# Moving the feature additions of an expert-routing stage, and one of three normalising steps of the last stage, to other engines

## The chip, the cores and the metric

The kernel runs on one core of a Trainium2 chip. Its time is the device time in microseconds of one execution. Three executions of the kernel before took 1827.47, 1829.99 and 1833.80 us, so the median is 1829.99 us. Engines are named as in the profile: PE is TensorE, DVE is VectorE, ACT is ScalarE, POOL is GpSimd, SP is SyncE. SP issues transfers only.

## What is computed

The input x is [8, 1024, 128] in float32: 8 batches of 1024 tokens. Two layers follow each other. Layer 0 is a recurrent mixer and a mixture of 8 experts. Layer 1 is a linear attention of three layers and a feed-forward part whose weight matrix depends on the token's position. The change touches the end of the two feed-forward parts. What they compute, shortened:

```
# layer 0, second half
h = layernorm(x) * (1 + cb) + sb                     # "feats"
eid   = argmax(h @ centroids.T)                      # the expert of each token
alpha = sigmoid(h @ centroids[e])
y     = h + relu(norm(h) @ w1[e] + b1[e]) @ w2[e] + b2[e]
x = x + gb * (alpha * y + (1 - alpha) * h)           # = x + gb*h + gb*alpha*(expert part)

# layer 1, second half
h = layernorm(x) * (1 + cb) + sb
idx = argmax over 8 tiles of the position scores     # one tile index for each position
y = h @ W[idx].T + b[idx]
x = x + gb * y
```

The term gb*h of the first half is the one that the change moves. It is independent of the experts' result, and is added to x in SBUF.

## The kernel before, in words

A batch is 8 chunks of 128 tokens (partition = token, 128 elements = channel). A half is 4 chunks, a tile of 128x512 elements. There are 16 halves.

**The expert stage**, function `experts`, is written out engine by engine in one block. The program on each engine is a fixed sequence. Engines meet only in semaphores. It has three phases:

- *Routing*, ten turns (b from -2 to 7), three batches in flight. PE turns the normalised rows (L1155) and computes affinities and transposes them back (L1162, L1164). ACT writes the features to `ex_feats` (L1105) and the normalised feature rows into a row buffer `ex_rows` (L1098). DVE picks the expert of each token and its place in a sorted list (L923 to L945). In each turn DVE also computes a shift (L905) for which ACT waits before L1098, copies gates (L918), and adds the features of half 0 of the batch before to x: `features_summed` (L950, L951). POOL scatters the rows of each batch to DRAM with eight indirect transfers (L1049).
- *The tile table.* From the final counts DVE computes which expert and which rows each of 71 tiles has (L980 to L998). At L987 it releases SP, which writes eight padding blocks (L1226), waits until all of these and all scatters have landed, and then loads one tile after another (L1234).
- *The tile loop*, 71 tiles. PE turns a tile (L1184), ACT scales it (L1132), PE multiplies by w1 (L1192) and w2 (L1199), ACT and DVE apply the ReLU (L1141, L1008), DVE forms the result (L1017, L1018), and POOL stores it by an indirect transfer (L1058). For each tile DVE copies the w1 of its expert into `ex_fT` (L1004) and thereby releases PE's L1192. The expert numbers come from registers that DVE loads from the table, 24 at a time.

Between table and loop DVE copies two w1 blocks and then does the other nine `features_summed`: half 1 of each batch, and half 0 of the last.

**The last stage**, inside `attention`, works on 8 batches of 10 rows of chunks (`ti_rows`), each in three parts of 4, 3 and 3 chunks (`PARTS`). ACT computes the reciprocal deviation of the next batch (L361, L362), DVE the shift (L1452), and ACT normalises the next batch's chunks in place, part after part (L1637), between its own modulations of the present batch (L1647). PE turns each part (L1902) and multiplies by the position's weights (L1914). DVE adds the bias (L1467) and computes the statistics of the batch after next (L1442, L1447). POOL scales the result (L1776), SP stores it, POOL gathers it back (L1783).

## Time and profile before

| | |
|---|---|
| time of the three executions | 1827.47, 1829.99, 1833.80 us |
| time of the profiled execution | 1829.99 us |
| its span, first to last instruction | 1828.0 us |
| PE busy | 1571.7 us (86%) |
| DVE busy | 1443.5 us (79%) |
| ACT busy | 935.3 us (51%) |
| POOL busy | 698.6 us (38%) |
| mean granted TensorE clock | 0.916 of full speed |

The profiled execution took the median time, and 1.99 us of it lie outside the span. The routing phase runs from about 213 to 333 us of the span, the tile loop from 356.9 to about 499 us, the attention until about 1742 us, and the last stage to the end. In a row of the timeline the first number is the start in us from the span's start and the second the busy time in us. At the end stands in brackets how long the engine was idle before it, and what released it. Busy time includes the time for which an instruction, once issued, is held up inside its engine.

### The profile page before, as it was taken

Reading aid. Unit: us, or ns where it says so; the run is one execution under the profiler, and the core shown is the slowest. Engines: PE = TensorE matmul, PEld = TensorE weight load, DVE = VectorE, ACT = ScalarE, POOL = GpSimd, SP = SyncE. Lnnn points to the kernel's source line nnn. Section 1 sums busy time; section 2 is a strip of 40 time slices with the busy share of each in tenths; the row PEclk is TensorE's granted clock in tenths of the full one; section 3 lists DMA queues with packets and bytes.
Section 4 is the critical chain, followed back from the end, with each engine's and each line's share of the span. In section 5 each row is a group of like instructions: output and inputs, shape, how many; then the busy total and the mean of one; then the engine's idle time right before and its main releaser. Section 6 shows DMA issues by size and latency. Waiting matters only on the chain.

```text
span 1828.0 us, 65037 instructions
## 1 busy us (share of the span) xinstructions
PE 1571.7 (86%) x27934; PEld 1150.5 (63%) x27934; DVE 1443.5 (79%) x3906; ACT 935.3 (51%) x1958; POOL 698.6 (38%) x620
## 2 busy tenths in 40 slices
PE   6777365399969999999999999999999999999853
PEld 4344254399946677776667777666677667777542
DVE  4998566766658888888888888888888988888864
ACT  4887476366524444445544444554444544444373
POOL 0777636345513234215224323423321522431354
PEclk9888655599969999999999999999999999999876
DMA  9730012333200000000000000100000000000437
GB/s 264 145 100 1 21 50 90 97 102 101 83 13 14 3 9 9 15 3 14 15 3 13 16 3 8 20 3 9 9 15 3 14 15 3 11 6 3 109 102 233
DMA packets 88606, 79.69 MB, mean 44 GB/s; under 512 B 22416, under 2 KB 77040, under 8 KB 88064
## 3 DMA queue, kind: packets, MB, share of 16 engines
q1 hardware_dynamic: 70736, 46.17, 9.6%
q0 software_dynamic: 10848, 25.70, 4.9%
q8 instruction: 221, 3.62, 0.9%
q10 hardware_dynamic: 6736, 3.66, 0.7%
q14 instruction: 65, 0.53, 0.1%
HBM read 46.74 MB, written 34.01 MB: 44 GB/s over the span
## 4 chain that ended last, share of the span: by engine, by line
PE 50%; DVE 13%; ACT 4%; issue 2%; DMA 1%; DVEq 1%; POOL 0%; another core or an unknown queue 0%; POOLq 0%; ACTq 0%
PE psum L1965 8%; PE psum L1890 8%; PE psum L1859 4%; PE psum L1868 4%; PE psum L1928 2%; PE psum L1934 2%; PE psum L1882 2%; PE psum L1936 2%; PE psum L1875 2%; PE psum L1937 2%; PE psum L1938 2%; PE psum L1948 2%; PE psum L1847 2%; DVE at_kb L1543 2%; PE psum L1929 2%
## 5 line engine op out<-in xcount | busy, mean ns | idle before, releaser
L1890 PE MATMUL psum<-attn_w,at_qa 128*128 128x128 f32 x1536 | 197.6, 282 | 0.0
L1752 POOL TENSOR_TENSOR at_xres<-at_xn,attn_rows 128x512 f32<-128x512 f32 x32 | 40.9, 1277 | 394.2 <-DVE at_xn L368 394.2
L1965 PE MATMUL psum<-at_vT,attn_w 128*128 128x512 f32 x384 | 180.6, 614 | 6.8 <-ACT at_vT L1697 5.8
L1890 PEld LDWEIGHTS psum<-attn_w,at_qa 128*128 128x128 f32 x1536 | 179.6, 192 | 6.1 <-issue 0.7
L1543 DVE TENSOR_SCALAR at_kb<-at_kf,const 128x512 f32<-128x512 f32 x192 | 178.4, 989 | 0.0
L1757 POOL TENSOR_TENSOR at_xn<-at_sqk,attn_rows 128x512 f32<-128x512 f32 x48 | 63.6, 1326 | 202.8 <-DVE at_sqk L368 202.8
L1549 DVE STREAM_TRANSPOSE at_vb<-at_vT 32x512 uint32<-32x512 uint32 x192 | 134.7, 701 | 1.9
L1669 ACT ACTIVATE at_qa<-at_qf,const 128x512 f32<-128x512 f32 x192 | 127.6, 714 | 1.6
L1713 ACT ACTIVATE at_qa<-psum,attn_bf 128x512 f32<-128x512 f32 x192 | 122.1, 678 | 10.6 <-PE psum L1965 5.4
L1565 DVE TENSOR_TENSOR at_weights<-psum,const 128x1024 f32<-128x1024 f32 x96 | 115.6, 1204 | 11.3 <-PE psum L1859 11.3
L361 ACT ACTIVATE at_rstd<-at_mv,const 128x4 f32<-128x4 f32 x96 | 28.1, 292 | 184.3 <-DVE at_mv L349 184.2
L1965 PEld LDWEIGHTS psum<-at_vT,attn_w 128*128 128x128 f32 x384 | 70.0, 192 | 82.2 <-issue 71.8
L1859 PE MATMUL psum<-at_qa,at_kb 64*64 64x64 f32 x6144 | 113.5, 224 | 9.5 <-issue 5.4
L1859 PEld LDWEIGHTS psum<-at_qa,at_kb 64*64 64x64 f32 x6144 | 100.5, 137 | 21.0 <-issue 9.9
L1868 PE MATMUL psum<-at_state,at_qa 64*64 64x36 f32 x3072 | 111.1, 242 | 0.0
L1868 PEld LDWEIGHTS psum<-at_state,at_qa 64*64 64x64 f32 x3072 | 106.3, 143 | 0.0
L1058 POOL DMA_INDIRECT token_y<-ex_y,ex_place x71 | 70.1, 988 | 85.3 <-DVE ex_y L1018 79.0
L1763 POOL TENSOR_TENSOR at_qf<-at_qf,ga_rows 128x512 f32<-128x512 f32 x16 | 20.3, 1271 | 207.8 <-DVE at_qf L368 207.8
L1847 PEld LDWEIGHTS psum<-at_v,at_kt 32*32 32x32 f32 x6144 | 62.1, 103 | 50.9 <-issue 49.4
L1049 POOL DMA_INDIRECT sorted_x<-ex_rows,ex_pos x64 | 63.2, 988 | 63.8 <-ACT ex_rows L1098 44.8
L346 DVE BATCH_NORM_STATS2 at_stats<-at_kt 128x6 f32<-128x128 f32 x384 | 83.8, 281 | 3.3
L1875 PE MATMUL psum<-at_vb,at_weights 128*32 128x36 f32 x6144 | 79.1, 201 | 8.1 <-issue 7.9
(308 smaller groups left out, 3884.2 us busy)
## 6 DMA issues: line engine op xcount, KB each, us to landing
ex_rows<-sorted_x SPq DMA_DIRECT2D x71, 129.0 KB
ti_rows<-tile_rows SPq DMA_DIRECT2D x8, 640.0 KB
x<-in_L_attn_x SPq DMA_DIRECT2D x8, 512.0 KB, 7.3
tile_rows<-in_L_attn_x SPq DMA_DIRECT2D x8, 512.0 KB
x<-token_y POOLq DMA_DIRECT2D x8, 512.0 KB
tile_y<-ti_rows SPq DMA_DIRECT2D x16, 192.0 KB
out<-x ACTq DMA_DIRECT2D x12, 256.0 KB
expert_w<-in_L_ffn_w SPq DMA_DIRECT2D x1, 2048.0 KB, 14.2
```

Source lines behind the costliest of these rows:

```text
L346: nc.vector.bn_stats(stats[:, c, :], x_of(c))
L1543: last = nc.vector.tensor_scalar(kb[s][:, :, b, :], kf[s][:].rearrange("p (j i) -> p j i", i=SUB), cst(k, "mask_b")[:, b:b + 1], None, ALU ...
L1549: last = nc.vector.transpose(vb[s][q, :, :, b, 0:DH].bitcast(U32), vT[s][q, :].bitcast(U32).rearrange("p (j a d) -> p j a d", a=HQ, d=DH))
L1565: nc.vector.tensor_tensor(weights[a.s][:, i, :, :, :, :].rearrange("p h j a i -> p (h j a) i"), pair(a.s, 1 - i).rearrange("p (g i) -> p g ...
L1669: last = nc.scalar.activation(qa[s][:, :, i, :], qf[s][:].rearrange("p (j i) -> p j i", i=SUB), ACT.Copy, scale=cst(k, "mask_a")[:, i:i + 1])
L1713: nc.scalar.activation(hidden[f.s][:, t, :], bank(f.s, t), ACT.Relu, bias=k.bf1[:, f.l, t:t + 1]).then_inc(hid_taken, 1)
L1847: last = mm(bank(s, j)[quad(r), c * GW:(c + 1) * GW], kt[s][quad(j), c, quad(r)], v1[s][quad(j), c, :, r, :], start=True, stop=True)
L1859: last = mm(pair(s, 1 - i)[half_of(e), h * G + j * P // 2:h * G + (j + 1) * P // 2], kb[s][half_of(h), g, 2 * e:2 * e + 2, :].rearrange("p ...
L1868: mm(bank(1 - s, 2 + g // 8)[half_of(h), g % 8 * GW:(g % 8 + 1) * GW], qa[s][half_of(h), g, 2 * h:2 * h + 2, :].rearrange("p a i -> p (a i)"),
L1875: last = mm(bank(1 - s, 2 + i)[quad(a), g % 8 * GW:(g % 8 + 1) * GW], weights[s][:, i, a // 2, g % 8, a % 2, :], vb[s][:, g, a, :, :].rear ...
L1890: last = mm(bank(f.s, 1)[:, c * D:(c + 1) * D], hidden[f.s][:, t, c * P:(c + 1) * P], k.w2[:, f.l, t, :], start=(t == 0 and c == 0), stop= ...
L1965: mm(bank(f.s, c), k.w1[:, f.l, c * P:(c + 1) * P], hT[f.s][:], start=True, stop=True).then_inc(hid_ready, 1)
```

## The change

In the expert stage `features_summed` is gone. DVE does 12 of the 16 halves (`BY_VECTOR`, batches 0 to 5) in one run behind the tile table, ahead of its register load and of the first w1 copies. POOL does the other four (batches 6 and 7) behind its last scatter and ahead of its first tile store.

In the last stage the third part of the next batch (three chunks) is normalised by DVE, as (row - mean) * rstd, instead of by ACT, for batches 1 to 7. PE waits for a semaphore of its own for that part.

```diff
+        BY_VECTOR = (NB - 2) * HALVES
...
-                def features_summed(b, h):
-                    f, x = (half_at(t, b * HALVES + h) for t in (feats, k.x))
-                    dve.wait_ge(rows_ready, b + 1)
-                    st.done(nc.vector.tensor_tensor(f, f, row_of(k.gb0[:, b, :]), ALU.mult))
-                    nc.vector.tensor_tensor(x, x, f, ALU.add).then_inc(f_added, 1)
...
-                    if real(b - 1):
-                        features_summed(b - 1, 0)
...
                 dve.wait_ge(tiles_ready, 1)
                 st.wait()
 
+                dve.wait_ge(rows_ready, BY_VECTOR // HALVES)
+                for g in range(BY_VECTOR):
+                    f, x = half_at(feats, g), half_at(k.x, g)
+                    st.done(nc.vector.tensor_tensor(f, f, row_of(k.gb0[:, g // HALVES, :]), ALU.mult))
+                    nc.vector.tensor_tensor(x, x, f, ALU.add).then_inc(f_added, 1)
...
                 weights(e[0], 0)
                 weights(e[1], 1)
-                for b in range(NB):
-                    features_summed(b, 1)
-                features_summed(NB - 1, 0)
                 last_hidden(0, e[0], 0)
...
+                def features_scaled(g):
+                    f = half_at(feats, g)
+                    st.mark(nc.gpsimd.tensor_tensor(f, f, row_of(k.gb0[:, g // HALVES, :]), ALU.mult))
+
+                def features_added(g):
+                    x = half_at(k.x, g)
+                    st.wait()
+                    nc.gpsimd.tensor_tensor(x, x, half_at(feats, g), ALU.add).then_inc(f_added, 1)
+
+                for g in range(BY_VECTOR, NB * HALVES):
+                    features_scaled(g)
+                    features_added(g)
                 for n in range(TILES):
                     store(n)
...
+                def last_part_normalised(n):
+                    for r in range(PARTS[-1].start, PARTS[-1].stop):
+                        last = nc.vector.tensor_scalar(rows[n][:, r, :], rows[n][:, r, :], t_mv[n % 2][:, r, 0:1], t_rstd[n % 2][:, r:r + 1],
+                                                       ALU.subtract, ALU.mult)
+                    last.then_inc(t_last_ready, 1)
...
                         tile_result(n * UNITS)
                         if n + 2 < NB:
                             tile_statistics(n + 2, range(0, TROWS // 2))
+                        if n + 1 < NB:
+                            last_part_normalised(n + 1)
                         tile_result(n * UNITS + 1)
...
-                                tile_normalise(n + 1, u)
+                                if u < UNITS - 1:
+                                    tile_normalise(n + 1, u)
...
-                    pe.wait_ge(t_xn_ready, i + 1)
+                    if n and u == UNITS - 1:
+                        pe.wait_ge(t_last_ready, n)
+                    else:
+                        pe.wait_ge(t_xn_ready, i + 1 - max(n - 1, 0))
```

How the instructions stand. On DVE, between the tile table and the tile loop, before (`ex_tile_at` is the table, `ex_fT` the w1 copies, TENSOR_LOAD the register load):

```order
L998 TENSOR_TENSOR ex_tile_at<-ex_tile_e,ex_tile_row 128x71
L879 TENSOR_LOAD ex_tile_at
L880 ISA x3
L1004 COPY ex_fT<-expert_w 128x512
L1004 ISA
L1004 COPY ex_fT<-expert_w 128x512
L950 TENSOR_TENSOR ex_feats<-ex_feats,gb_rows 128x512
L951 TENSOR_TENSOR x<-x,ex_feats 128x512
```

The last two rows stand nine times. The same place with the change (line numbers are shifted there: L991 is the old L998, L1003 the old L1004, L998 and L999 are the multiply and the add):

```order
L991 TENSOR_TENSOR ex_tile_at<-ex_tile_e,ex_tile_row 128x71
L998 TENSOR_TENSOR ex_feats<-ex_feats,gb_rows 128x512
L999 TENSOR_TENSOR x<-x,ex_feats 128x512
L879 TENSOR_LOAD ex_tile_at
L880 ISA x3
L1003 COPY ex_fT<-expert_w 128x512
L1003 ISA
L1003 COPY ex_fT<-expert_w 128x512
```

The multiply and the add stand twelve times, and the w1 copies, which PE waits for, are now behind all of them. On POOL behind the last scatter, with the change (L1045 is the scatter, the old L1049, and L1054 the tile store, the old L1058):

```order
L1045 DMA sorted_x<-ex_rows,ex_pos 67456x258 x7
L1059 TENSOR_TENSOR ex_feats<-ex_feats,gb_rows 128x512
L1064 TENSOR_TENSOR x<-x,ex_feats 128x512 [waits ex_pool_steps]
L1059 TENSOR_TENSOR ex_feats<-ex_feats,gb_rows 128x512
L1064 TENSOR_TENSOR x<-x,ex_feats 128x512 [waits ex_pool_steps]
L1054 DMA token_y<-ex_y,ex_place 10112x128 [waits ex_y_ready] x71
```

The pair stands four times in all. Before, the store followed the scatter directly. On DVE in one round of the last stage, with the change (L1481 adds the bias, the old L1467; L1450 are the statistics, the old L1442; L1473 is new):

```order
L1481 TENSOR_TENSOR ti_rows<-psum,ti_bias 128x512 [waits ti_y_ready]
L1450 BN_STATS ti_stats<-ti_rows 128x6 [waits rows_by_queue2]
L1450 BN_STATS ti_stats<-ti_rows 128x6 x4
L1473 TENSOR_SCALAR ti_rows<-ti_rows,ti_mv,ti_rstd 128x128 x3
L1481 TENSOR_TENSOR ti_rows<-psum,ti_bias 128x384 [waits ti_y_ready]
```

Three instructions are added between the first statistics and the second bias addition of each of seven rounds. Everything else on DVE keeps its order there.

## Rows read from the trace of the kernel before

**Rows 1.** The timeline of one routing turn: start, busy, engine, line, operation, idle before.

```profile
290.20 0.21 ACT L362 ACTIVATE ex_frstd<-ex_frstd 128x8 f32<-128x8 f32 x1
291.45 0.13 DVE L905 SCALAR_TENSOR_TENSOR ex_fshift<-ex_fmv,ex_frstd 128x8 f32<-128x8 f32 x1
292.49 3.19 ACT L1098 ACTIVATE ex_rows<-ex_feats,ex_fshift,ex_frstd 128x128 f32<-128x128 f32 x8 [2.08 <-DVE ex_fshift L905]
295.92 0.28 DVE L923 COPY ex_aff<-psum 128x32 f32<-128x32 f32 x2
```

**Rows 2.** The timeline, DVE's L923 in two other turns.

```profile
270.90 0.29 DVE L923 COPY ex_aff<-psum 128x32 f32<-128x32 f32 x2 [1.14 <-PE psum L1164]
312.09 0.29 DVE L923 COPY ex_aff<-psum 128x32 f32<-128x32 f32 x2 [6.50 <-remote]
```

**Rows 3.** The timeline of DVE from the tile table to the tile loop.

```profile
338.96 0.23 DVE L998 TENSOR_TENSOR ex_tile_at<-ex_tile_e,ex_tile_row 128x71 int32<-128x71 f32 x1
342.36 0.77 DVE L1004 COPY ex_fT<-expert_w 128x512 f32 x2 [3.17 <-issue]
343.05 0.68 DVE L950 TENSOR_TENSOR ex_feats<-ex_feats,gb_rows 128x512 f32<-128x512 f32 x1
354.39 0.69 DVE L951 TENSOR_TENSOR x<-x,ex_feats 128x512 f32<-128x512 f32 x1
```

**Rows 4.** The timeline of POOL, SP and PE at the start of the tile loop.

```profile
344.87 1.02 POOL L1049 DMA_INDIRECT sorted_x<-ex_rows,ex_pos  x1 [0.30 <-issue]
353.39 5.91 SPq L1234 DMA_DIRECT2D ex_rows<-sorted_x  x6
356.89 1.91 PE L1192 MATMUL psum<-ex_xsT,ex_fT 128*128 128x128 f32 x8
362.91 0.96 POOL L1058 DMA_INDIRECT token_y<-ex_y,ex_place  x1 [17.02 <-DVE ex_y L1018]
```

**Rows 5.** Busy time by stretch, one stretch of the tile loop: us, each engine, clock, DMA.

```profile
380.00:400.00 20.00, 20.00 (x182) 20.00 (x182) 14.86 (x54) 14.35 (x44) 10.52 (x11) 1.00 0.42 108
```

**Rows 6.** The timeline at the end of the mixer: DVE and POOL, both with operands in SBUF.

```profile
204.56 1.26 POOL L727 TENSOR_TENSOR mx_t<-mx_t 128x512 f32<-128x512 f32 x1
204.76 1.60 DVE L538 SCALAR_TENSOR_TENSOR mx_den<-mx_er,mx_den 128x512 f32<-128x512 f32 x1
205.90 1.60 POOL L731 TENSOR_TENSOR mx_rw<-mx_t,mx_den 128x512 f32<-128x512 f32 x1
207.45 1.26 POOL L727 TENSOR_TENSOR mx_t<-mx_t 128x512 f32<-128x512 f32 x1
```

**Rows 7.** Four L1543 and one POOL operation (timeline); all L1543 (min/median/max ns).

```profile
558.80 2.43 POOL L1809 TENSOR_TENSOR ga_rows<-ga_rows,attn_rows 128x1024 f32<-128x1024 f32 x1
553.99 7.52 DVE L1543 TENSOR_SCALAR at_kb<-at_kf,const 128x512 f32<-128x512 f32 x4
L1543 DVE TENSOR_SCALAR at_kb<-at_kf,const x192: 472/1114/2578, 531.8 to 1701.3; 128x512 f32<-128x512 f32 x192
```

**Rows 8.** The timeline of one round of the last stage.

```profile
1775.76 0.93 DVE L1452 SCALAR_TENSOR_TENSOR ti_shift<-ti_mv,ti_rstd 128x10 f32<-128x10 f32 x1 [0.17 <-ACT ti_rstd L362]
1776.72 1.65 ACT L1637 ACTIVATE ti_rows<-ti_rows,ti_shift,ti_rstd 128x128 f32<-128x128 f32 x4 [1.00 <-DVE ti_shift L1452]
1777.37 1.27 POOL L1776 TENSOR_TENSOR ti_rows<-ti_rows,gb_rows 128x512 f32<-128x512 f32 x1 [0.70 <-DVE ti_rows L1467]
1780.42 0.56 DVE L1467 TENSOR_TENSOR ti_rows<-psum,ti_bias 128x384 f32<-128x384 f32 x1 [2.16 <-PE psum L1914]
1782.03 0.77 DVE L1447 BATCH_NORM_AGGREGATE ti_mv<-ti_stats 128x2 f32<-128x6 f32 x10
1782.84 0.30 ACT L361 ACTIVATE ti_rstd<-ti_mv,const 128x10 f32<-128x10 f32 x1 [0.36 <-DVE ti_mv L1447]
```

**Rows 9.** The timeline: the shortest wait before that L1467, and four DVE normalising steps.

```profile
1764.87 0.56 DVE L1467 TENSOR_TENSOR ti_rows<-psum,ti_bias 128x384 f32<-128x384 f32 x1 [0.95 <-PE psum L1914]
1740.98 1.11 DVE L368 TENSOR_SCALAR at_qf<-at_kt,at_mv,at_rstd 128x128 f32<-128x128 f32 x4 [0.60 <-ACT at_rstd L362]
```

More of the change, by code:

```diff
@@ L1314, in attention @@
         t_ = lambda name: m.sem("ti_" + name)
-        (weights_ready, bias_loaded, t_stats_ready, t_rstd_ready, t_shift_ready, t_xn_ready, t_xT_ready, t_hT_ready,
+        (weights_ready, bias_loaded, t_stats_ready, t_rstd_ready, t_shift_ready, t_xn_ready, t_last_ready, t_xT_ready, t_hT_ready,
          y_ready, y_biased, y_scaled, y_last, x_done) = (t_(n) for n in (
-             "weights_ready", "bias_loaded", "stats_ready", "rstd_ready", "shift_ready", "xn_ready", "xT_ready", "hT_ready",
+             "weights_ready", "bias_loaded", "stats_ready", "rstd_ready", "shift_ready", "xn_ready", "last_ready", "xT_ready", "hT_ready",
              "y_ready", "y_biased", "y_scaled", "y_last", "x_done"))
```

## The prediction, made before the changed kernel was run

> **What bounds the kernel now.** I went from the page (PE 86% busy) to the timeline of the two stages that the change touches, and looked there for the wait that ends last.
>
> *Routing.* DVE has a dense stretch in one turn: its L905 at 291.45 us comes 1.04 us after ACT's deviation was ready (290.20 + 0.21 = 290.41), and ACT waits for it [rows 1]. In that turn L923 follows L951 without a wait, so the moved pair pushes DVE. In most other turns L923 waits after the pair, for PE (1.14 us) or in a longer stall (6.50 us) [rows 2], and the pair is covered.
>
> *Start of the tile loop.* The table is done at 338.96 + 0.23 = 339.19 us. The register load takes until the first w1 copy at 342.36, so 3.17 us. The nine pairs of multiply and add run from 343.05 to 355.08 [rows 3]: 12.03 / 18 = 0.668 us an instruction. They are hidden: the w1 copies stand ahead of them, POOL's last scatter ends at 345.89, SP's first load goes out at 353.39, and PE's first L1192 starts at 356.89 [rows 4]. That chain runs over SP. DVE is off it.
>
> *Tile loop.* PE is busy for 20.00 of 20 us, DVE for 14.86 [rows 5]. Whatever delays the first L1192 arrives whole at the end of the loop, and the attention behind it starts when all engines are through.
>
> *Last stage.* ACT looks like its bound, but the round closes over DVE: shift, ACT's first part (1776.72), its modulation, PE's product, DVE's L1467 (1780.42), statistics, aggregation until 1782.80, ACT's L361 at 1782.84 after an idle time of 0.36 us, the next shift [rows 8]. The third part that ACT normalises is not in this chain.
>
> **The change part by part.**
>
> 1. *Seven pairs leave the routing turns.* The dense turn gains the 1.04 us by which L905 was late; the last turn gains a whole pair before the table, 2 x 0.668 = 1.34 us; the others nothing. ACT's L1098 started only 0.91 us after L905 had ended (291.58 to 292.49 [rows 1]), in a pause that no row explains. If that went too, the gain would be 1.95 instead of 1.04; if the stalls absorb it, 0. I take 1.04. Table done: 339.19 - 2.38 = 336.81. SP's first load, which hangs on the same counts, could go out at 351.01, and PE could start at 354.5.
>
> 2. *Twelve pairs now stand ahead of the register load and of the w1 copies.* 24 x 0.668 = 16.03 us, so 352.84 if nothing disturbs them. Then 3.17 for the registers and 0.43 for the first copy (two take 0.77): 356.44. That is only 0.45 us earlier than before, and already later than the 354.5 of SP's chain. DVE becomes the last to arrive.
>
> 3. *POOL's four pairs run against them.* POOL's last scatter ends at 345.89 - 1.04 = 344.85; DVE then has (352.84 - 344.85) / 0.668 = 12 instructions left, POOL begins eight of its own. Both kinds have all their operands in SBUF. What two such streams do to each other is shown at the end of the mixer [rows 6]: POOL's L727 runs from 204.56 to 205.82; DVE's operation, issued at 204.76, takes 1.60 instead of about 0.67 (an instruction of that size in rows 3) and ends 0.54 after POOL's; POOL's next, issued at 205.90, takes 1.60 instead of 1.26. They exclude each other. A stream of several is shown too: four L1543, 0.472 us each when undisturbed, took 7.52 us beside a series of POOL operations like the one of 2.43 [rows 7]. DVE gets one instruction in for each of POOL's, back-to-back or not. POOL's own spacing is 1.28 on average without DVE (1.26 and a gap of 0.08 behind each multiply, half of the time, less a small overlap) and 0.33 more with it (1.60 less its usual 1.27): 1.61. Eight rounds take 12.9 us, in which DVE does eight instructions worth 5.34. The delay is 12.9 - 5.3 = 7.6 us. Its lower bound is 0, no exclusion. Its upper bound is a whole POOL operation for each, 8 x 1.27 = 10.2.
>
>    First w1 copy ready at 356.44 + 7.6 = 364.0, so PE's first L1192 at 364.0 instead of 356.89: **+7.1 us** (-0.5 to +9.7, and another +1.0 or -0.9 from step 1).
>
>    On this the Trainium skill has a rule (SBUF — State Buffer, section "Who interferes with whom"): a DVE instruction with two SBUF inputs contends with a GpSimd instruction that reads SBUF, and the one that issues second blocks for the whole of the other. Rows 6 agree in kind, since DVE ends only after POOL. By the letter of the rule each of the eight would wait the full 1.27 us, and the sum would be +9.7; the row's 1.60 for a POOL operation shows that part of its start overlaps with DVE's. The same page says that a `tensor_tensor` does not starve the writing of descriptors, so twelve of them beside POOL's last scatters should not slow these; no row of mine tests a long run of them.
>
> 4. *POOL's first tile store* was due at 362.91 [rows 4]. POOL is through at 344.85 + 12.9 = 357.8, and the store itself comes 7 us later. Nothing behind it waits. Cost 0. If POOL were late, eight result buffers would still cover it.
>
> 5. *Last stage, ACT.* Seven times 1.26 us leave ACT; ACT waits for DVE anyway [rows 8]. Gain 0; the most it could be is 7 x 1.26 = 8.8.
>
> 6. *Last stage, DVE.* Three steps of 128x128 more in seven rounds: four such take 1.11 us from the first to the last end, with starts 0.26 apart [rows 9], so three 0.85. They stand where DVE idles for 2.16 us before the second L1467 [rows 8]; the shortest of these waits is 0.95 [rows 9]. POOL's L1776 runs there at the same time, and may hold them until 1778.64; 1778.64 + 0.85 = 1779.5 is still before 1780.42. In the round with the short wait they may reach 0.3 us beyond it. Cost: **+0.3 us** (0 to 7 x 0.85 = 6).
>
>    Sum: 7.1 + 0.3 = 7.4 us. The profiled execution took 1829.99, which is also the median: **1837.4 us**.
>
> **Rivals.**
>
> A. *The two streams hardly hold each other up.* DVE would be alone, w1 ready at 356.4, and the stage would gain 0.45 us. With 0.3 lost at the end: 1829.8. For it: the moved additions have never run beside POOL arithmetic in this trace. Against: rows 6 and 7.
>
> B. *ACT is the bound of the last stage after all.* Then it gains up to 8.8 us, 1.26 a round, and the kernel would be at 1837.4 - 9.1 = 1828.3; with A as well at 1820.7. This is the case on the other side. Its place is ACT's stretch between two L1452, its price 1.26 a round; it decides as soon as L361 doesn't wait for L1447. For it: in the round of 1775.76 DVE's L1452 took 0.93 for 10 elements a partition, since POOL's L1776 was in its way; if ACT's earlier end moves that meeting, 0.76 a round comes on top. Against: the 0.36 us of idle time before L361, with the third part still in ACT's sequence.
>
> C. *POOL wins more often, or the steps of the last stage are pushed out of their cover.* 9.7 for the start, 2 to 4 for the last stage: 1842 to 1844.
>
> D. *The routing shrinks by more*, because all DVE work of a turn becomes shorter and the long stalls go too: up to 7 x 1.34 = 9.4 us instead of my 2.4. It would pull DVE's run and POOL's forward together: 1830.4 to 1835. Against: rows 2.
>
> **How the numbers follow.** My forecast 0.66, own range 1834.5 to 1840; A 0.10; B, alone or with A, 0.09; C 0.08; D 0.07. The range for 8 in 10 leaves out the far end of C and most of B: 1829.5 to 1842. A difference of 0.3%, 5.5 us, is about what can be told from none here, so the borders are at 1824.5 and 1835.5. The forecast lies 1.9 us above the upper one, and its range crosses it: of its 0.66 I give 0.50 to slower and 0.16 to same. C goes to slower. A and D go mainly to same, B about half to faster. Slower 0.58, same 0.33, faster 0.09.
>
> **What would show it.** In the profile after: the table done about 2.4 us earlier; DVE's last eight or so multiply-adds ahead of the loop at 1.2 to 1.9 us instead of 0.67, POOL's eight at up to 1.6; PE's first L1192 near 364, released by DVE's w1 copy and not by a load; the end of the loop later by the same 7 us; in the last stage an idle time of ACT before L361 of more than 1 us, and rounds as long as before. I am wrong if DVE's instructions keep 0.67 beside POOL's, if PE's first product waits for its rows and not for w1, or if the last stage becomes shorter.

## The result and the profile after

The changed kernel takes 1841.84 us (median of 7 executions, 1839.55 to 1844.91). The kernel before took 1829.99 us beside it (7 executions, 1825.66 to 1836.63). The ratio is 1.006 [1.0047, 1.0075]: 11.85 us slower. The forecast was 1837.4, slower by 7.4, in a range of 1829.5 to 1842.0. The direction was right, the size was short by 4.4 us; the upper bound of the range held by 0.16 us.

| | before | after |
|---|---|---|
| profiled execution, its span | 1829.99, 1828.0 us | 1845.99, 1844.1 us |
| PE, DVE busy | 1571.7, 1443.5 us | 1572.4, 1456.0 us |
| ACT, POOL busy | 935.3, 698.6 us | 927.7, 710.8 us |
| mean granted TensorE clock | 0.916 | 0.915 |

The profiled execution lies 4.2 us above the median of its kernel, so its span differs by more (16.1 us) than the medians do.

The timeline of DVE in the changed kernel, from the routing to the tile loop (start, busy, engine, line, operation, idle before and what ended it). L924 is the old L923, L991 the old L998, L1003 the old L1004:

```profile
302.78 0.29 DVE L924 COPY ex_aff<-psum 128x32 f32<-128x32 f32 x2 [10.71 <-remote]
...
326.93 0.29 DVE L924 COPY ex_aff<-psum 128x32 f32<-128x32 f32 x2 [4.82 <-remote]
...
342.61 0.23 DVE L991 TENSOR_TENSOR ex_tile_at<-ex_tile_e,ex_tile_row 128x71 int32<-128x71 f32 x1
342.88 0.71 DVE L998 TENSOR_TENSOR ex_feats<-ex_feats,gb_rows 128x512 f32<-128x512 f32 x1
...
348.93 2.05 DVE L999 TENSOR_TENSOR x<-x,ex_feats 128x512 f32<-128x512 f32 x1
350.91 1.74 DVE L998 TENSOR_TENSOR ex_feats<-ex_feats,gb_rows 128x512 f32<-128x512 f32 x1
352.68 1.63 DVE L999 TENSOR_TENSOR x<-x,ex_feats 128x512 f32<-128x512 f32 x1
...
360.92 1.75 DVE L998 TENSOR_TENSOR ex_feats<-ex_feats,gb_rows 128x512 f32<-128x512 f32 x1
362.70 0.69 DVE L999 TENSOR_TENSOR x<-x,ex_feats 128x512 f32<-128x512 f32 x1
...
366.68 0.69 DVE L999 TENSOR_TENSOR x<-x,ex_feats 128x512 f32<-128x512 f32 x1
369.37 0.76 DVE L1003 COPY ex_fT<-expert_w 128x512 f32 x2 [2.00 <-issue]
```

Against [rows 3]: the table is done at 342.84 (before 339.19), and the first w1 copy starts at 369.37 (before 342.36). Eight of the 24 instructions between take 1.63 to 2.05 us, the other sixteen 0.68 to 0.71. The same timeline on the other engines, with L1045 the old L1049, L1242 the old L1234, L1192 the old L1184 and L1200 the old L1192:

```profile
348.11 1.02 POOL L1045 DMA_INDIRECT sorted_x<-ex_rows,ex_pos  x1 [0.30 <-issue]
349.15 1.27 POOL L1059 TENSOR_TENSOR ex_feats<-ex_feats,gb_rows 128x512 f32<-128x512 f32 x1
350.50 1.60 POOL L1064 TENSOR_TENSOR x<-x,ex_feats 128x512 f32<-128x512 f32 x1
352.06 1.70 POOL L1059 TENSOR_TENSOR ex_feats<-ex_feats,gb_rows 128x512 f32<-128x512 f32 x1
...
360.52 1.59 POOL L1064 TENSOR_TENSOR x<-x,ex_feats 128x512 f32<-128x512 f32 x1
340.15 10.46 SPq L1234 DMA_DIRECT2D sorted_x<-ex_spare  x8
353.23 5.91 SPq L1242 DMA_DIRECT2D ex_rows<-sorted_x  x6
355.44 0.47 PE L1192 MATMUL psum<-const,ex_rows 128*128 128x128 f32 x1 [25.77 <-DMA ex_rows<-sorted_x]
369.95 2.04 PE L1200 MATMUL psum<-ex_xsT,ex_fT 128*128 128x128 f32 x8 [12.98 <-DVE ex_fT L1003]
```

Against [rows 4]: the rows of the first tile arrive as before (SP's first load 353.23, before 353.39). PE turns them at 355.44 and then waits 12.98 us for DVE's copy. Its first product starts at 369.95 instead of 356.89, 13.06 us later. The last result of the loop starts at 513.14 instead of 499.71, 13.43 later, so the delay arrives whole.

In the last stage the idle time of ACT before its L361 (start of the reciprocal deviation), over seven rounds, grouped by line (count, busy us, mean ns, idle us and its releasers), before and then after:

```profile
L361 ACT ACTIVATE ti_rstd<-ti_mv,const 128x10 f32<-128x10 f32 x7 | 2.1, 302 | 3.3 <-DVE ti_mv L1447 2.4 <-issue 0.9
```

```profile
L361 ACT ACTIVATE ti_rstd<-ti_mv,const 128x10 f32<-128x10 f32 x7 | 2.1, 303 | 6.7 <-DVE ti_mv L1455 5.6 <-issue 1.1
```

ACT was relieved of 18 steps there (29.1 to 21.5 us) and waits more for DVE. From the first bias addition to the last the stage takes 57.58 us before (1744.90 to 1802.48) and 57.07 after (1760.56 to 1817.63): no difference in these two traces.

### The profile page after: what moved, and what is told of

It reads as the page before. It is cut to its first block, busy times and chain, and to the rows that moved or that the text cites. A ratio compares the mean times of both kernels' runs of the same rounds, so it can differ in the third digit from the quotient of the medians.

```text
span 1844.1 us, 65037 instructions
## 1 busy us (share of the span) xinstructions
PE 1572.4 (85%) x27934; PEld 1151.9 (62%) x27934; DVE 1456.0 (79%) x3919; ACT 927.7 (50%) x1937; POOL 710.8 (39%) x628
## 4 chain that ended last, share of the span: by engine, by line
PE 53%; DVE 11%; ACT 4%; issue 2%; DMA 1%; DVEq 0%; POOL 0%; POOLq 0%; another core or an unknown queue 0%; ACTq 0%
PE psum L1985 9%; PE psum L1907 8%; PE psum L1876 5%; PE psum L1885 4%; PE psum L1948 2%; PE psum L1954 2%; PE psum L1899 2%; PE psum L1956 2%; PE psum L1864 2%; PE psum L1958 2%; PE psum L1957 2%; PE psum L1968 2%; PE psum L1892 2%; PE psum L1949 2%; PE psum L1857 2%
## 5 line engine op out<-in xcount | busy, mean ns | idle before, releaser
L1730 ACT ACTIVATE at_qa<-psum,attn_bf 128x512 f32<-128x512 f32 x192 | 122.4, 678 | 10.9 <-PE psum L1985 6.6
L361 ACT ACTIVATE at_rstd<-at_mv,const 128x4 f32<-128x4 f32 x96 | 28.1, 292 | 186.8 <-DVE at_mv L349 186.8
L1876 PEld LDWEIGHTS psum<-at_qa,at_kb 64*64 64x64 f32 x6144 | 100.7, 137 | 23.2 <-issue 12.2
L1054 POOL DMA_INDIRECT token_y<-ex_y,ex_place x71 | 70.2, 989 | 82.4 <-DVE ex_y L1017 75.3
L1200 PE MATMUL psum<-ex_xsT,ex_fT 128*128 128x128 f32 x568 | 77.5, 280 | 14.1 <-DVE ex_fT L1003 13.0
L1045 POOL DMA_INDIRECT sorted_x<-ex_rows,ex_pos x64 | 63.1, 986 | 68.3 <-ACT ex_rows L1106 48.7
```

Source lines behind the costliest of these rows:

```text
L1200: last = nc.tensor.matmul(o, w1[q % 2][:, t * P:(t + 1) * P], xsT[q % 2][:], start=True, stop=True)
L1730: nc.scalar.activation(hidden[f.s][:, t, :], bank(f.s, t), ACT.Relu, bias=k.bf1[:, f.l, t:t + 1]).then_inc(hid_taken, 1)
L1876: last = mm(pair(s, 1 - i)[half_of(e), h * G + j * P // 2:h * G + (j + 1) * P // 2], kb[s][half_of(h), g, 2 * e:2 * e + 2, :].rearrange("p ...
```

## The experiments

Twelve versions ran in three sets of four (e1 to e4, e5 to e8, e9 to e12), and one point is needed to read them. In the first measurement and in the last set the kernel before took 1830 us; in the two sets between it took 1798.89 and 1800.44 us. Each ratio is against the kernel before on the same chip in the same set. The chip does not explain the two levels: e1 to e4 and e9 to e12 ran on the same one, e5 to e8 on another. Losses in us are differences of the medians, unless they are said to go by the ratio. The traces say where 16 to 26 of those 30 us lie: in the sets between, the routing has none of the idle stretches in which PE, ACT and DVE stand still together ([rows 2], where DVE's wait is 6.50 us and "remote"; 10.71 above). Those of more than 1.5 us make 10.6 us in the trace of before and 22.3 in that of e9. I call the traces without them undisturbed. The starts below are read from the timelines; "turns" is from the first L923 to the eighth, "last stage" from the first bias addition to the last.

| trace | turns | table done | first w1 product | last result of the loop | last stage |
|---|---|---|---|---|---|
| before | 95.7 | 339.19 | 356.89 | 499.71 | 57.6 |
| after | 98.4 | 342.84 | 369.95 | 513.14 | 57.1 |
| e1 expert stage only | 79.5 | 320.36 | 347.34 | 490.49 | 50.0 |
| e2 last stage only | 79.5 | 322.77 | 335.66 | 478.74 | 55.0 |
| e3 copies first | 79.5 | 320.42 | 334.26 | 491.10 | 54.8 |
| e4 all pairs on DVE | 79.4 | 320.65 | 344.59 | 487.49 | 55.4 |
| e5 the change again | 79.4 | 321.64 | 348.62 | 491.99 | 55.0 |
| e6 last stage, steps late | 79.4 | 322.62 | 335.94 | 478.84 | 51.0 |
| e7 eight pairs each | 79.4 | 320.78 | 337.47 | 481.93 | 55.3 |
| e8 twelve pairs in turns | 80.1 | 321.38 | 335.61 | 478.18 | 49.2 |
| e9 before again | 104.3 | 346.86 | 365.53 | 511.30 | 55.3 |
| e10 eight pairs in turns | 105.1 | 346.32 | 364.56 | 509.52 | 57.4 |
| e11 before, held 2 us | 99.0 | 344.74 | 358.51 | 502.25 | 54.8 |
| e12 changed, held 2 us | 101.0 | 344.85 | 371.96 | 515.98 | 56.3 |

**e1, the expert stage alone.** The change without its last-stage part:

```diff
-                                if u < UNITS - 1:
-                                    tile_normalise(n + 1, u)
+                                tile_normalise(n + 1, u)
```

and `last_part_normalised` with its call and semaphore taken out. Expected:

> The change's expert stage alone; the last stage is that of the kernel before. Theory: all of the loss lies in the expert stage. The profile of the changed kernel has TensorE's first product with w1 at 369.95 us where the kernel before has it at 356.89 (+13.1), and the stages behind it lose no more by design, so that this version comes out as the changed kernel: 1841.8 us, 1.006 of the time before, and the first product again near 370. Rival: the last stage has a share of the loss (its VectorE steps beside the other work); then this version is 2 to 4 us faster than the changed kernel. Second question, on the turns of the routing: the prediction had the tile table done at 336.8 and the profile showed it at 342.84, later than before (339.19). If that is what seven pairs fewer do to the turns, it comes again here; if it is where TensorE's long idle stretches with no releaser happened to fall (9.76 us before one product of turn 5), the table moves by some us from one version to the next.

Measured: 1.0073 [1.0056, 1.0089], 13.1 us by the ratio and 14.5 by the medians. The main loss is in the expert stage, but not all of it: the rival is right, since beside e5's 1.01 this version is 4 to 5 us faster than the whole change. The second question is answered: the turns take 79.5 us, and the 3.65 us by which the table was late in the first profile do not come again.

**e2, the last stage alone.** The kernel before with `last_part_normalised` and what belongs to it. Expected:

> The change's last stage alone: the third part of each next batch normalised by VectorE, the expert stage as in the kernel before. Theory of the prediction: no effect (+0.3, between -8.8 and +6): 1830, ratio 1.000. Rival: ScalarE's 24 us of steps were on the path, ratio 0.997 to 0.9955; or VectorE's steps are, ratio 1.001 to 1.003. The routing turns here hold the same instructions as the kernel before, so its table should be done at 339.2 again, first product at 356.9; how far it isn't is the spread that one profile has.

Measured: 1.0031 [1.002, 1.0042], 5.6 us: not the theory's nothing, and just above the rival's range. The expert stage of this trace has the form of before, undisturbed: its turns are as long as e1's although each has a pair in it. DVE in three rounds of its last stage (timeline; L1465 are the new steps, L1473 the bias additions, L1452 the shift):

```profile
1726.87 0.95 DVE L1465 TENSOR_SCALAR ti_rows<-ti_rows,ti_mv,ti_rstd 128x128 f32<-128x128 f32 x3
...
1733.11 3.54 DVE L1465 TENSOR_SCALAR ti_rows<-ti_rows,ti_mv,ti_rstd 128x128 f32<-128x128 f32 x3
1736.56 0.54 DVE L1473 TENSOR_TENSOR ti_rows<-psum,ti_bias 128x384 f32<-128x384 f32 x1
...
1738.15 0.79 DVE L1447 BATCH_NORM_AGGREGATE ti_mv<-ti_stats 128x2 f32<-128x6 f32 x10
1738.86 0.53 DVE L1473 TENSOR_TENSOR ti_rows<-psum,ti_bias 128x384 f32<-128x384 f32 x1
1739.55 0.93 DVE L1452 SCALAR_TENSOR_TENSOR ti_shift<-ti_mv,ti_rstd 128x10 f32<-128x10 f32 x1 [0.17 <-ACT ti_rstd L362]
...
1741.97 1.06 DVE L1465 TENSOR_SCALAR ti_rows<-ti_rows,ti_mv,ti_rstd 128x128 f32<-128x128 f32 x3
```

and POOL at the same time:

```profile
1731.62 4.42 POOL L1785 TENSOR_TENSOR ti_rows<-ti_rows,gb_rows 128x512 f32<-128x512 f32 x4
```

The second set of steps falls on four scaling operations of POOL and takes 3.54 us instead of 0.95. The bias addition behind it starts without a wait, so the cover of 0.95 to 2.16 us that the prediction counted on [rows 8, 9] is used up, and statistics, means and shift come late. Over the stage (L361 grouped by line, in e1 and then in e2):

```profile
L361 ACT ACTIVATE ti_rstd<-ti_mv,const 128x10 f32<-128x10 f32 x8 | 2.4, 302 | 2.7 <-DVE ti_mv L1455 2.6
```

```profile
L361 ACT ACTIVATE ti_rstd<-ti_mv,const 128x10 f32<-128x10 f32 x8 | 2.4, 302 | 9.6 <-DVE ti_mv L1447 9.6
```

ACT waits 9.6 us for the means where it waited 2.7. Not all of this is loss, since ACT also has less to do. Its normalising, over the same window, in e1 and then in e2:

```profile
L1645 ACT ACTIVATE ti_rows<-ti_rows,ti_shift,ti_rstd 128x128 f32<-128x128 f32 x80 | 33.3, 484 | 3.3 <-DVE ti_shift L1460 3.3
```

```profile
L1645 ACT ACTIVATE ti_rows<-ti_rows,ti_shift,ti_rstd 128x128 f32<-128x128 f32 x59 | 24.4, 482 | 4.8 <-DVE ti_shift L1452 4.8
```

It works 8.9 us less. Its waits for the means, the shifts and PE's products together grow from 7.2 to 20.6 us, so by 13.4: 4.5 more than it was relieved of, near the 5.0 by which the stage is longer in e2 than in e1.

**e3, copies first.** `Experts`, the register load and the first two w1 copies ahead of the twelve pairs:

```diff
-                dve.wait_ge(rows_ready, BY_VECTOR // HALVES)
-                for g in range(BY_VECTOR):
...
                 weights(e[0], 0)
                 weights(e[1], 1)
+                dve.wait_ge(rows_ready, BY_VECTOR // HALVES)
+                for g in range(BY_VECTOR):
...
```

Expected:

> The changed kernel with the experts' register load and the first two w1 copies ahead of VectorE's twelve pairs, not behind them. TensorE's first product then waits for rows and not for VectorE: 355 to 357 us again. But VectorE is in its pairs until 342.84 + 3.6 + 24.5 = 371 (GpSimd's four beside them), and the first hidden step on VectorE, which TensorE needs for its second product with w2, comes behind them (in the kernel before it started at 358.98). Theory (what counts is when VectorE is through with its pairs, wherever the copies are): the stream of tiles starts 371 - 359 = 12 us late, less two tiles that are ready ahead (TensorE's first two products, about 3.7 us in the trace): 8 us slower than before, 3 to 4 us faster than the changed kernel, about 1838. Rival: the copies' place was the whole loss, and two buffers of w1 and of hidden rows carry TensorE over it: 1829 to 1831.

Measured: 1.0093 [1.0077, 1.0109], within the noise the loss of the whole change (1.01 in e5). PE's timeline:

```profile
334.26 1.92 PE L1200 MATMUL psum<-ex_xsT,ex_fT 128*128 128x128 f32 x8
335.97 0.42 PE L1192 MATMUL psum<-const,ex_rows 128*128 128x128 f32 x1
336.19 1.92 PE L1200 MATMUL psum<-ex_xsT,ex_fT 128*128 128x128 f32 x8
349.99 1.22 PE L1207 MATMUL psum<-expert_w,ex_xn 128*128 x4 [11.89 <-DVE ex_xn L1001]
```

PE begins 1.4 us earlier than in e2 and is stopped two products later, by the hidden step of DVE, which is queued behind the pairs. The theory had this, but counted 3.7 us for the two products and so 3 to 4 us less than the whole change; the loop ends 12.4 us later than in e2, 0.9 earlier than in e5. What counts is when DVE is through with its pairs. Its rival is refuted.

**e4, no pairs on POOL.**

```diff
-        BY_VECTOR = (NB - 2) * HALVES
+        BY_VECTOR = NB * HALVES
```

Expected:

> The changed kernel with all sixteen pairs on VectorE, none on GpSimd, at the same place ahead of the copies. Theory: nine of VectorE's operations took 1.63 to 2.05 us instead of 0.68 because GpSimd's eight ran beside them, and each engine waited for the other. Then sixteen pairs alone take 16 x 1.37 = 21.9 us where twelve took 24.49 with GpSimd beside them: the first product with w1 comes 2.6 us EARLIER although VectorE does a third more: 367.4 if the table is done at 342.8, ratio to the kernel before 1.0045 instead of 1.006. Rival (the slow operations come from the loads and stores that start at about 349, not from GpSimd): four more pairs lengthen the run by at least 5.3 us, 29.8 or more: ratio 1.009 or more. No operation of the run over 0.75 us: theory; a stretch at 1.6 us again: rival.

Measured: 1.0064 [1.005, 1.0079]. The timeline of DVE and PE:

```profile
341.32 0.69 DVE L999 TENSOR_TENSOR x<-x,ex_feats 128x512 f32<-128x512 f32 x1
344.01 0.76 DVE L1003 COPY ex_fT<-expert_w 128x512 f32 x2 [2.00 <-issue]
344.59 1.83 PE L1200 MATMUL psum<-ex_xsT,ex_fT 128*128 128x128 f32 x7 [9.62 <-DVE ex_fT L1003]
```

All 32 instructions take 0.69 us or less and end at 342.01. Sixteen pairs alone take 21.3 us; twelve beside POOL's four took 24.4 in e1. With a third more work on DVE the first product comes 2.75 us earlier (2.6 expected). The mutual hold-up is shown, and loads as its cause are refuted. The ratio was expected at 1.0045; that figure was made from the first measurement's 1.006, and in the undisturbed sets the change costs more (e5).

**e5, the change again.** Expected:

> The changed kernel once more, beside the three single-part versions. In the four runs so far TensorE had none of the idle stretches without a releaser that stood in its first stages in the first two profiles (5.46 and 6.64 us before, 5.59 and 9.76 us after): turns of 11.2 and 11.5 us throughout, with and without the seven pairs, and the table at 322.54 with them, 320.13 to 320.42 without. Where the parts were timed apart, the expert stage alone cost 13.1 us (1.0073) and the last stage alone 5.6 us (1.0031). Theory: they add up, as they lie in stages one behind the other: 1.0104, table at 320.3, first product with w1 at 347.3. Rival: the last stage's loss is hidden or given back when both are made, and the ratio is the 1.006 to 1.0075 of the first measurement.

Measured: 1.01 [1.0084, 1.0116], 18.8 us by the medians and 18.0 by the ratio. Within the noise the parts add up: 0.73% and 0.31% against 1.00%. In this set the same code costs 7 us more than in the first measurement.

**e6, the steps late.** The last stage alone, with the steps in another place:

```diff
-                        if n + 1 < NB:
-                            last_part_normalised(n + 1)
                         tile_result(n * UNITS + 1)
                         if n + 2 < NB:
                             tile_statistics(n + 2, range(TROWS // 2, TROWS))
                             tile_means(n + 2)
+                        if n + 1 < NB:
+                            last_part_normalised(n + 1)
```

Expected:

> The last stage alone, as in the run where it cost 5.6 us, but with VectorE's three steps of the next batch's third part behind the means of the batch after it, not between the first half of its statistics and the second. Theory: the loss came from the place. There the steps (0.34 us alone, up to 1.5 us beside GpSimd's scaling; mean 562 ns, 9.2 us in all for 18) stand ahead of statistics, means, deviation and shift, and ScalarE waited 7.3 us in the stage for the means where it waited 0.6 with the old form. Behind the means they delay only the next result; ScalarE is relieved of its 24 steps, so the stage is as before or shorter: ratio 0.997 to 1.0005. Rival: what costs is that VectorE has the steps at all (9.2 us more of an engine that shares its rounds with GpSimd's scaling), wherever they stand: 1.002 to 1.004, and ScalarE waits as long for the means of the next round.

Measured: 1.0019 [1.0009, 1.0029], 2.8 us. That is above the theory's range and at the lower edge of the rival's. The trace, of an execution 2.0 us faster than the median, is nearer to the theory: the stage takes 51.0 us, where the early steps gave 54.8 to 55.4 and the old form 49.2 and 50.0. The steps, and the shift, grouped by line:

```profile
L1465 DVE TENSOR_SCALAR ti_rows<-ti_rows,ti_mv,ti_rstd 128x128 f32<-128x128 f32 x21 | 7.6, 428 | 0.0
L1452 DVE SCALAR_TENSOR_TENSOR ti_shift<-ti_mv,ti_rstd 128x10 f32<-128x10 f32 x8 | 1.3, 161 | 1.8 <-ACT ti_rstd L362 1.8
```

In e2 the same lines took 11.4 and 4.4 us. ACT still waits 8.2 us for the means, as the rival had it, but its waits together are 16.1 us, 8.9 more than in e1 and just what it was relieved of. By the traces some 4 of the 5.5 us lost in the stage (55.1 against 49.6, the means of five and two traces) were the place; by the times of e2 and e6 it is 2 to 3 us, and their intervals overlap, so this share is likely and not settled. It is in any case no gain: relieving ACT buys nothing in the two places tried.

**e7, eight pairs each.** `BY_VECTOR = NB * HALVES // 2`. Expected:

> The changed kernel with eight pairs on VectorE and eight on GpSimd, where the change has twelve and four. Theory (one operation of each engine at a time, about 1.67 us for one of VectorE's and one of GpSimd's that meet, and each engine's turn after the other's): GpSimd begins some 8.2 us after VectorE, at about 328.6. VectorE has twelve of its sixteen operations behind it by then, four meet GpSimd's: 8.2 + 4 x 1.67 = 14.9 us instead of 24.4, free at 335.3, first product with w1 at about 338 to 340 instead of 347.3. But GpSimd has twelve more operations to go, beside the copies and the first tiles' steps, each of which may be held by up to 1.3 us until about 350, and its first store waits behind them (TQ results are in flight before VectorE waits for a store). Forecast 1.002 to 1.005. Rival (beside GpSimd VectorE loses by time, not by operations met, or the first stores' delay stops the tiles): 1.007 or more.

Measured: 1.0045 [1.003, 1.006], with the last stage's part in it. The timeline of DVE:

```profile
328.18 0.69 DVE L999 TENSOR_TENSOR x<-x,ex_feats 128x512 f32<-128x512 f32 x1
328.79 2.04 DVE L998 TENSOR_TENSOR ex_feats<-ex_feats,gb_rows 128x512 f32<-128x512 f32 x1
330.87 1.64 DVE L999 TENSOR_TENSOR x<-x,ex_feats 128x512 f32<-128x512 f32 x1
332.43 1.75 DVE L998 TENSOR_TENSOR ex_feats<-ex_feats,gb_rows 128x512 f32<-128x512 f32 x1
334.21 1.64 DVE L999 TENSOR_TENSOR x<-x,ex_feats 128x512 f32<-128x512 f32 x1
336.90 1.83 DVE L1003 COPY ex_fT<-expert_w 128x512 f32 x2 [1.04 <-issue]
339.69 0.35 DVE L1007 TENSOR_SCALAR ex_xn<-psum,expert_b 128x128 f32<-128x128 f32 x1 [0.97 <-PE psum L1200]
339.96 1.52 DVE L1003 COPY ex_fT<-expert_w 128x512 f32 x1
```

Exactly the last four of sixteen meet POOL, as the count of met operations says. The first product is at 337.47, a little before the forecast. POOL's pairs go on until 352 and hold the w1 copies instead (1.52 us; 0.42 alone, as in e2), yet the loop ends only 3.2 us later than in e2. Twice as many pairs on POOL delay the loop's end by a quarter of what the four do (13.3 us in e5), because fewer meet DVE's run and PE waits for that run.

**e8, twelve pairs in the turns.** The kernel before with

```diff
-                    if real(b - 1):
+                    if 0 <= b - 1 < NB - 2:
                         features_summed(b - 1, 0)
+                        features_summed(b - 1, 1)
...
-                for b in range(NB):
-                    features_summed(b, 1)
-                features_summed(NB - 1, 0)
+                for b in (NB - 2, NB - 1):
+                    features_summed(b, 0)
+                    features_summed(b, 1)
```

Expected:

> The kernel before, with both halves of batches 0 to 5 added in the routing turns (twelve pairs), none in the last turn, and four pairs behind the w1 copies where nine stood. Its last stage is that of before. Theory: turns of 11.2 and 11.5 us were the same with a pair in them and without, VectorE 9.7 busy with one, so a second pair (1.34 us) just fits: the table is done 2.3 us earlier as in the changed kernel's runs (320.3), and VectorE, which in the run with before's expert stage was through with its nine pairs at 339.3 and let the second w2 product wait, is free at about 331: the stream of tiles starts with its rows at about 334.3 instead of 335.7 and without that wait: 3 us gained, ratio 0.9983. Rival: a second pair makes turns longer (11.05 busy of 11.35 leaves nothing for the waits inside a turn), by up to 1.3 us in each of six: 1.000 to 1.004.

Measured: 0.9991 [0.9982, 1.0], 2.35 us faster at the median, at the border of what can be told. Seven turns take 80.1 instead of 79.4 us, the first product comes no earlier (335.61), and the loop ends 0.6 us earlier. The expected 3 us are not there. It is the only version that is not slower than the kernel before.

**e9, the kernel before again**, profiled with one timed execution. Expected:

> The kernel before, once more, for its trace beside the single-part versions. Expected as put together from them: turns of 11.2 and 11.5 us, table done at 322.4, first product with w1 at 335.7, and a last stage of 49 to 50 us from its first result to its last (49.2 and 50.0 in the two versions that have its form, 57.6 in the first profile). If the last stage takes 55 to 58 us here too, then what the last-stage edit costs isn't the 5.3 us that the traces with and without it differ by.

Measured: 1842.04 us, above the 1823.53 to 1838.0 of the 24 other executions, so only its trace is used. The set turned out to be of the disturbed kind (turns of 104.3 us), and the last stage took 55.3 us. So the old form of the stage has no fixed length: 49.2 and 50.0 undisturbed, 57.6, 55.3 and (e10) 57.4 disturbed. The new form has 54.8 to 55.4, and 57.1 and 56.3.

**e10, eight pairs in the turns.** As e8, but the second half only for batches 0 and 2, and eight pairs behind the copies. Expected:

> The kernel before with only as many pairs moved forward as VectorE needs: six first halves and two second halves (batches 0 and 2) in the turns, none in the last turn, eight pairs behind the w1 copies where nine stood. With twelve in the turns four turns became 0.1 to 0.4 us longer, the last scatter came no earlier (328.5) and only VectorE's run was out of the way; with eight the turns lose 0.2 to 0.4 us in all. Theory: table near 320.5, last scatter near 327.7, first product with w1 at about 334.7 instead of 335.7, VectorE free at 336 to 337 instead of 339.3, when its first hidden step is due: the stream of tiles 2 to 2.5 us earlier: ratio 0.9987. Rival: the gain is under the 0.1% that five rounds show: 0.9995 to 1.0005.

Measured: 1.0025 [1.0008, 1.0042], slower, which neither side had. Its trace has the first product 0.97 and the loop's end 1.8 us earlier than e9, and the last stage 2.1 longer. What the loss consists of is open.

**e11, before, held up once.** Ten repeated statistics steps (behind a drain) in round 0:

```diff
                             tile_means(n + 2)
+                        if n == 0:
+                            nc.vector.drain()
+                            tile_statistics(2, range(TROWS))
```

Expected:

> The kernel before with ten statistics steps repeated on VectorE (about 2.1 us) in the first round of the last stage, ahead of the result of batch 0's third part. In the first profile VectorE came to that result 2.08 us late, after an idle stretch without a releaser; the shift behind it met GpSimd's scaling and took 1.74 us, and later rounds took 7.7 to 8.2 us where undisturbed ones take 6.5 to 7.2. Theory: the stage has a fast and a slow rhythm; one delay of 2 us moves VectorE's shift under GpSimd's scaling, and the rounds behind it stay longer: the stage grows from 49.5 to 55 to 58 us, ratio 1.003 to 1.0045. Rival: the delay costs itself alone or less, since rounds behind it run as before: at most 2.1 us, ratio 1.000 to 1.0012.

Measured: 1.0025 [1.0005, 1.0044]; the stage in the trace takes 54.8 us. This test did not decide: it was made for an undisturbed stage, and in this set the old form was at 55.3 and 57.4 without it. The interval holds both sides' figures.

**e12, the changed kernel, held up once.** The same lines. Expected:

> The same ten steps in the changed kernel (ratio to the kernel before without them: 1.010). Theory: with VectorE's three normalising steps in it the stage is in the slow rhythm already (55.0 to 55.4 us in four traces), so a delay of 2.1 us adds no more than itself: 1.010 to 1.0115. Then, in a process in which such stretches strike both kernels, the last-stage edit costs nothing over before, and the change as a whole is left with the expert stage's 1.0065 to 1.0075, near the 1.006 first measured. Rival (the two add up): 1.013 or more.

Measured: 1.0068 [1.0044, 1.0092], less than either side had. With 2 us of work added the whole change still costs 12.3 us here, as in the first measurement, against 18.8 in e5's set.

## Why the prediction was right or wrong

*Step 1, the routing: this is the step that failed.* The table was forecast at 336.81 and came at 342.84. The gain has two parts. The last turn's pair is worth what was said: from the eighth L923 to the table done 13.8 and 14.0 us with it (e2, e6), 12.5 and 12.7 without (e5, e1). The 1.04 us of the dense turn is not there: seven turns take 79.5 us with the pairs and without. I had taken a turn of 12.5 us with DVE without a wait [rows 1] as bound by DVE, but the changed kernel has such a turn too (269.89 to 282.37, with DVE waiting 0.76 us for PE at its end). In the first two profiles the 1.3 us drowned in the idle stretches, which make seven turns 95.7 to 105.1 us long in six traces where undisturbed ones take 79.4 to 80.1; in the changed kernel they were 2.7 us longer, and the last turn was late as well (ACT's L1106 idle for 3.43 us before 334.78, though the shift that it waits for ended at 333.41). These stretches are larger than the term that I worked out to a hundredth.

*Steps 2 and 3, right.* From table done to first product the prediction had 364.0 - 336.81 = 27.19 us. The trace has 369.95 - 342.84 = 27.11, e12 27.11, e1 and e5 26.98. Inside it the run of pairs is 24.49 (forecast 16.03 + 7.6 = 23.6), POOL's eight operations take 12.96 (12.9), and the registers 2.00 instead of 3.17. That the sum fits to 0.1 us is partly luck: the run is 0.9 us longer than forecast, the register load 1.2 shorter, and no run explains the latter. The hold-up is 24.49 - 16.03 = 8.5 us for eight POOL operations. The Trainium skill's rule (SBUF — State Buffer, "Who interferes with whom"), by which the second blocks for the whole of the first, would have made it 10.2; the trace agrees in kind. In amount it falls short of that: one operation of each engine takes 1.67 us together, where 0.67 and 1.28 one behind the other would be 1.95, so a part of each overlaps. With the other statement of that page of the Trainium skill, that a `tensor_tensor` does not starve the writing of descriptors, the trace agrees: POOL's last scatter takes 1.02 us beside DVE's run, and in e9 scatters take 0.96 us while DVE stands still (282.7 to 291.5).

*The cover that this is set against was taken as fixed, and it is not.* The same stretch, table done to first product, is 17.70 us in the first profile of before, 18.67 in e9, 13.77 in e11, 12.89 in e2 and 13.32 in e6. SP's eight padding stores make part of it: 14.11 us in the profile of before, 10.46 in that of after, 8.33 in e2. In the profile of before SP's first load goes out 2.60 us after the last of them; in e2 POOL's last scatter ends later than they do (329.59), and the load goes out 2.53 us after that. In e2:

```profile
320.29 8.33 SPq L1226 DMA_DIRECT2D sorted_x<-ex_spare  x8
335.66 1.91 PE L1192 MATMUL psum<-ex_xsT,ex_fT 128*128 128x128 f32 x8
```

So the expert stage costs 27.0 less this cover less 1.3: 12.4 to 12.8 us undisturbed (e1 and e5 against e2 and e6 in the traces: 12.2), and 8.0 with the cover of the profile that I had. The first measurement's 11.85 lies between.

*Step 4, right.* POOL stands ready for 13.65 us before its first store (375.76), and in e7, with eight operations more on POOL before it, the loop was not stopped.

*Step 5, right.* ACT's relief gained nothing. Its idle time before L361 grew to 6.7 us.

*Step 6, right for the first measurement, wrong as a rule.* Forecast +0.3, and 57.6 against 57.1 us in the first two traces. Undisturbed it is +5.5 in the traces and +5.6 in the median, near the upper bound of 6. I had allowed for POOL's scaling once a round; a set of three steps can meet three operations (3.54 us).

*The rivals.* A fell with e4. B fell: the stage never became shorter by more than its own spread. C had the right size (1842), but its main reason is wrong: the hold-up is 8.5 us and not 10.2. Its other reason, steps pushed out of their cover, is what the undisturbed runs show. D fell: seven pairs less shrink no turn. The chances did not quite add up as told: with B about half to faster, faster would have had 0.05 and not 0.09.

*Taken together:* 13.4 of the profile's 16.1 us are there at the end of the tile loop. Another 2.2 come between it and the first bias addition (15.66 later, less the 13.43), the last stage gives 0.5 back, and 1.0 comes behind it. The attention's length varies from trace to trace, 1239.7 us in e4 and 1245.0 in e7, which have the same code there, so the 2.2 need no cause in the change. That the time fell into the range owes much to the set of runs: the sum held against the long cover of 17.70 us. Undisturbed the same change costs 18.8 us, two and a half times the forecast's 7.4, and three terms make 10.9 of the 11.4 us between: 4.6 us of cover (12.9 to 13.3 in place of 17.7), 1.1 of the routing's gain and 5.2 in the last stage.

What stays open: what the idle stretches are, and whether they move the last stage into its long form or something else does. Of the stretches the traces show this much: PE, ACT and DVE stop behind a finished product of PE (before, 307.13), no releaser is recorded, and ACT and DVE then start at the same moment what waits for PE's products (both 312.09). POOL does not stop: its scatters go on through the 9.38 us of e9's longest stretch (282.63 to 292.00).

## What to carry to other kernels

Work moved off a busy engine is only gained if that engine was the last to arrive there: read the wait behind the moved instructions in several turns, not in one. Work moved ahead of a copy that another engine waits for is paid in full, less whatever else is late at that point, and that cover should be read from more than one trace. Before giving elementwise work with SBUF operands to GpSimd, count how many of its operations will meet a run on VectorE: each cost that run about 1.05 us here, and it was cheaper to do all the work on VectorE alone.

## What the runs showed of the hardware

- 128x512 float32 additions and multiplications in SBUF on VectorE (0.67 us alone) and GpSimd (1.27 us) alternate when they meet: 1.63 to 1.75 us on the one, 1.59 to 1.71 on the other, the first meeting 2.05. A w1 copy of 0.42 us took 1.52, and a shift of 10 elements a partition 0.93 instead of 0.17.
- Ahead of the loop PE's granted clock is 0.50, which is 1.2 GHz, both while it idles and before, in the last turns of the routing (e1, 300 to 322: PE busy for 7.56 of 22 us). The loop's first products of eight take 1.9 us instead of 1.06. In e1, by stretches (busy PE, PEld, DVE, ACT, POOL, clock, DMA share, GB/s):

```profile
335.00:347.00 12.00, 0.00 (x0) 0.00 (x0) 9.87 (x10) 0.23 (x1) 6.41 (x4) 0.50 0.20 56
347.30:352.50 5.20, 5.16 (x24) 5.19 (x25) 1.66 (x6) 2.11 (x7) 0.00 (x0) 0.50 0.00 0
352.60:362.00 9.40, 9.40 (x84) 9.40 (x84) 6.44 (x23) 6.04 (x18) 4.13 (x5) 0.98 0.29 68
```

  The kernel before starts its loop with the same duration (first product 1.91 us [rows 4]), and from the first product to the last result of the loop both kernels take nearly the same time (142.8 and 143.2 us), so the clock makes no more than a small part of the difference.
- The same kernel takes 1830 us in one set of runs and 1800 in another, on one and the same chip (e1 to e4 against e9 to e12), and the same change costs 11.9 or 18.8 us. A ratio of one set is not the ratio of the next.
